# Inner values in a PSUM bank of their own, keys and y in one bank, and another order of accumulates, expert pieces and first tiles

## What is computed

```python
x = x + wkv(w, u, layernorm(x), ctx)     # a weighted running mean of ctx, weights exp(key)
h = layernorm(x)
shared = sigmoid(h @ sg.T) * ((silu(h @ Wg.T) * (h @ Wu.T)) @ Wd.T)     # inner width 1024
routed = sum over the 2 best of 8 experts of prob * expert(h)           # inner width 256 each
out = x + shared + routed
```

## Time and profile before

| | us |
|---|---|
| runs (3): median, lowest, highest | 590.62, 587.41, 590.75 |
| the profiled execution's own time | 590.7 |
| its span, first to last instruction | 588.8 |
| PE busy | 484.0 (82%) |
| DVE busy | 437.7 (74%) |
| POOL busy | 345.4 (59%) |
| ACT busy | 277.5 (47%) |
| mean granted TensorE clock | 0.96 of full speed |

### The profile page before, as it was taken

How to read it: one execution, slowest core, us unless ns; L and a number is a source line. 1 busy time by engine, 2 the same in 40 slices (tenths; PEclk the granted TensorE clock), 3 DMA queues, 4 the chain that set the end, 5 groups by cost and what they waited for, 6 DMA issues and landing times.

```text
span 588.8 us, 11209 instructions
## 1 busy us (share of the span) xinstructions
PE 484.0 (82%) x3293; PEld 319.8 (54%) x3293; DVE 437.7 (74%) x954; ACT 277.5 (47%) x534; POOL 345.4 (59%) x422
## 2 busy tenths in 40 slices
PE   0126828999899799899797998899999999999980
PEld 0025615766676677576575666555555555555530
DVE  5968787898989989989989677558665666666650
ACT  4687335357376375384573465543332323332320
POOL 5964346755857848848858264642455755565332
PEclk9999768999999999899899999999999999999995
DMA  7961111021322314213230501043547866766452
GB/s 284 409 255 37 40 32 36 20 90 38 127 91 73 131 50 159 76 56 127 72 125 7 162 20 48 2 127 73 103 85 140 146 113 114 128 119 111 89 72 36
DMA packets 25932, 59.21 MB, mean 101 GB/s; under 512 B 6314, under 2 KB 6314, under 8 KB 24338
## 3 DMA queue, kind: packets, MB, share of 16 engines
q0 software_dynamic: 9824, 20.90, 20.0%
q1 hardware_dynamic: 16050, 37.59, 17.9%
HBM read 37.83 MB, written 20.65 MB: 99 GB/s over the span
## 4 chain that ended last, share of the span: by engine, by line
PE 34%; DVE 24%; issue 12%; ACT 8%; DMA 6%; POOL 2%; SPq 1%; POOLq 0%; ACTq 0%; DVEq 0%
PE GU L956 13%; PE GU L995 6%; PE DN L971 6%; PE DN L1011 5%; DMA out<-wall,cb 5%; DVE hx L1313 3%; DVE wall L1192 3%; PE XT L902 3%; DVE st L1195 2%; DVE wall L1185 2%; ACT wall L736 2%; DVE th L1306 2%; DVE th L1308 1%; ACT wall L658 1%; PE YT L902 1%
## 5 line engine op out<-in xcount | busy, mean ns | idle before, releaser
L995 PE MATMUL GU<-xt,wall 128*128 128x256 f16 x1536 | 193.1, 279 | 4.8 <-DVE xt L1217 2.4
L995 PEld LDWEIGHTS GU<-xt,wall 128*128 128x128 f16 x1536 | 153.0, 101 | 40.3 <-issue 5.2
L1011 PE MATMUL DN<-wall,hx 128*128 128x512 f16 x384 | 100.0, 399 | 28.5 <-DVE xb L1320 16.1
L614 POOL DMA_INDIRECT out<-wall,cb x39 | 62.0, 1590 | 81.5 <-SPq L386 39.6
L683 ACT ACTIVATE th<-GU,scl 128x256 f32<-128x256 f32 x103 | 48.5, 471 | 107.3 <-PE GU L995 58.3
L1011 PEld LDWEIGHTS DN<-wall,hx 128*128 128x128 f16 x384 | 36.9, 101 | 69.5 <-issue 25.3
L1313 DVE TENSOR_TENSOR hx<-th,hx 128x256 f16<-128x256 f32 x64 | 47.6, 744 | 27.2 <-ACT hx L692 26.3
L1306 DVE SCALAR_TENSOR_TENSOR th<-th,GU 128x256 f32<-128x256 f32 x103 | 41.9, 407 | 31.4 <-ACT th L683 31.1
L956 PE MATMUL GU<-wall,kb 128*128 x240 | 61.4, 379 | 0.2 <-issue 0.2
L956 PE MATMUL GU<-wall,xnb 128*128 x228 | 58.5, 379 | 0.4 <-DVE xnb L1516 0.4
L971 PE MATMUL DN<-wall,hx 128*128 x234 | 56.9, 379 | 1.0 <-DVE hx L1313 1.0
(11 more groups left out here) (164 smaller groups left out, 809.1 us busy)
## 6 DMA issues: line engine op xcount, KB each, us to landing
wall<-wgu SPq DMA_DIRECT2D x12, 1024.0 KB, 7.7
wall<-wd SPq DMA_DIRECT2D x12, 512.0 KB, 8.5
out<-xb SPq DMA_DIRECT2D x20, 256.0 KB
xb<-x SPq DMA_DIRECT2D x16, 256.0 KB, 2.9
cb<-ctx_t SPq DMA_DIRECT2D x16, 256.0 KB
xn_rows<-xnb SPq DMA_DIRECT2D x16, 256.0 KB
xb<-xn_rows,cb POOLq DMA_INDIRECT x39
out<-wall,cb POOLq DMA_INDIRECT x39
```

Of the source, the lines that this page charges most:

```text
L614: pool.indirect_dma_start(out, bass.IndirectOffsetOnAxis(ap=idsa[:, j:j + 1], axis=0), ye[j % RESULTS], None, compute_op=ALU.add).then_inc ...
L995: ins = nc.tensor.matmul(GU[n % 2][:, g * 2 * P:(g + 1) * 2 * P], gate_up(sh_base(u // 2), wp, c)[:, f:f + P], xt_pair(n // PU * 2, xp, c) ...
L1011: ins = nc.tensor.matmul(DN[a][:], hx[n % 2][:, hp * IE + a * P:hp * IE + (a + 1) * P], down(sh_base(u // 2), wp, u % 2), start=u == 0 and ...
```

## The change

- A bank HS takes the inner values of the shared units: the second instruction of `hidden` writes HS instead of th, `unit_hi` and `hidden_lo` read HS. The slots' transposed inner values go to HS too. `unit_tanh` of a shared unit waits for `hidden` of unit n-2 instead of its `hidden_lo`.
- KT and YT are one bank. `keys_t` therefore waits for the residual of the tile before, `y_back` for the keys of the tile after. Tile 2's keys go to DN0.
- In the turns: `accumulate` stands right behind `residual_and_stats`; `keys_t` follows unit n+1 instead of unit n; `unit_hi(n+3)` stands behind the first expert piece of its own turn instead of at the head of the next turn. In turn 4 `y_back(3)` follows the first unit instead of standing inside it.
- The opening is in another order on all four engines.
- In the last shared groups some expert pieces and squares change places with `unit_hi`, and the low weights of expert 6 are made by DVE (two instructions) instead of POOL (three).

The diff, cut to its core (indentation shortened):

```diff
@@ -183,10 +183,14 @@
-KT, YT, XT, LG = bank("KT"), bank("YT"), bank("XT"), bank("LG")
+YT, XT, LG, HS = bank("YT"), bank("XT"), bank("LG"), bank("HS")
 GU = [bank("GU0"), bank("GU1")]
 DN = [bank("DN0"), bank("DN1")]
-HT = YT
+KT, HT = YT, HS
+
+def kt(t):
+    return DN[0] if t == 2 else KT
+
@@ -519,23 +523,20 @@
+    quotient(1)
...
-    quotient(1)
...
-    shared_d_lo(0)
...
+    shared_d_lo(0)
...
-    pool.wait_ge(nd, 4)
+    shared_d_lo(1)
...
-    shared_d_lo(1)
@@ -567,25 +568,23 @@
-    scatter(B - 4)
...
+    scatter(B - 4)
...
+    scales(E, E - 2)
+    scatter(B - 2)
...
-    scales(E, E - 2)
-    scatter(B - 2)
...
-    for k in range(3):
-        expert_lo(E - 2, k)
@@ -679,7 +678,7 @@
         act.wait_ge(gu, n + 1)
-        wait_from(act, h_lo, n - 1)
+        wait_from(act, h_rdy if n < N_EXP + 2 else h_lo, n - 1)
         nc.scalar.activation(th[par][:], GU[par][:, 0:IE], ACT.Tanh, scale=scale(row, TANH)).then_inc(tanh, 1)
@@ -689,7 +688,7 @@
         wait_from(act, dn, n - 1)
-        nc.scalar.activation(hx[par][:, 0:IE], th[par][:] if n < N_EXP else HT[:, 0:IE],
+        nc.scalar.activation(hx[par][:, 0:IE], HS[:, 0:IE] if n < N_EXP else HT[:, 0:IE],
                              ACT.Copy).then_inc(h_hi, 1)
...
@@ -750,45 +752,44 @@
-    first_norm(2)
...
+    first_norm(2)
+    expert_square(0, 0)
...
+    both_exps(2)
...
-    both_exps(2)
-    for k in range(3):
-        expert_square(0, k)
...
+    first_norm(3)
...
-    first_norm(3)
-    shared_d_split(0)
...
+    expert_square(0, 1)
...
-    shared_gu_hi(2)
+    shared_d_split(0)
...
+    shared_gu_hi(2)
+    unit_hi(1, 1)
+    shared_d_split(1)
...
+    unit_tanh(2, 0, SHARED)
...
-    shared_d_split(1)
-    unit_hi(1, 1)
...
-    unit_tanh(2, 0, SHARED)
...
-    both_exps(4)
-    first_norm(5)
...
+    both_exps(4)
+    first_norm(5)
+    unit_hi(3, 1)
+    expert_square(0, 2)
...
-        unit_hi(n - 1, 1)
@@ -815,10 +816,14 @@
-            for k in range(4):
+            expert_piece(hi_e, 0)
+        if ws_e is not None:
+            expert_piece(ws_e, 4)
+        unit_hi(n + 3, 1)
+        if hi_e is not None:
+            for k in range(1, 4):
...
-            expert_piece(ws_e, 4)
...
@@ -877,16 +880,18 @@
+    unit_hi(n + 2, 0)
...
-    unit_hi(n + 2, 0)
...
+    unit_hi(n + 3, 1)
...
-        unit_hi(N_EXP + j - 1, (N_EXP + 1 + r) % 2)
+        if j > 0:
+            unit_hi(N_EXP + j - 1, (N_EXP + 1 + r) % 2)
@@ -905,11 +910,14 @@
         wait_from(pe, kp1, t)
-        transposes(KT, kb, HC, k_t)
+        if t != 2:
+            wait_from(pe, x1_rdy, t - 1)
+        transposes(kt(t), kb, HC, k_t)
...
         wait_from(pe, x1_rdy, t)
+        pe.wait_ge(kp1, min(t + 2, B))
         transposes(YT, wkv(t, 3), HC, y_t)
@@ -1038,10 +1046,10 @@
+    sum_squares(1, 2 * SU + 1, 0)
...
-    sum_squares(1, 2 * SU + 1, 0)
+    y_back(1)
...
-    y_back(1)
@@ -1054,12 +1062,16 @@
     shared_units(0, beside={1: [first_turn_1], 2: [first_turn_2], 3: [lambda: xn_t_(2)]},
-                 beyond={0: [lambda: keys_t(3)]})
+                 between={0: [lambda: keys_t(3)]})
...
         def beside_0():
+            if i == LAG + 1:
+                y_back(i - 1)
             pe.wait_ge(listed, (i - 4) * LIST_STEPS + 2)
...
+
+        def beside_1():
             if i + 1 < B:
@@ -1069,7 +1081,7 @@
-        shared_units(j, between={0: [lambda: y_back(i - 1)]}, beside={0: [beside_0], 2: [beside_2]})
+        shared_units(j, between={0: [lambda: y_back(i - 1)]} if i > LAG + 1 else {}, beside={0: [beside_0], 1: [beside_1], 2: [beside_2]})
@@ -1132,7 +1144,7 @@
-            pe.wait_ge(last_lo, 1)
+            pe.wait_ge(last_lo, 2)
@@ -1167,7 +1180,7 @@
-        TT(wkv(t, 1), KT[:], growth[:], ALU.subtract).then_inc(kp1, 1)
+        TT(wkv(t, 1), kt(t)[:], growth[:], ALU.subtract).then_inc(kp1, 1)
@@ -1287,15 +1300,14 @@
-    def last_expert_lo(k):
...
-        e = E - 1
+    def last_expert_lo(e, k):
...
-            dve.wait_ge(w_hi, 3 * E)
+            dve.wait_ge(w_hi, 3 * e + 3)
...
-            dve.wait_ge(w_hi, 1 + 3 * E)
+            dve.wait_ge(w_hi, 3 * e + 4)
@@ -1305,12 +1317,12 @@
         dve.wait_ge(a1, n + 1)
-        STT(th[par][:], th[par][:], scale(row, KAPPA), GU[par][:, IE:2 * IE], ALU.mult,
+        STT(HS[:, 0:IE] if n < N_EXP else th[par][:], th[par][:], scale(row, KAPPA), GU[par][:, IE:2 * IE], ALU.mult,
             ALU.mult).then_inc(h_rdy, 1)
...
         dve.wait_ge(h_hi, n + 1)
-        TT(hx[par][:, IE:2 * IE], th[par][:] if n < N_EXP else HT[:, 0:IE], hx[par][:, 0:IE],
+        TT(hx[par][:, IE:2 * IE], HS[:, 0:IE] if n < N_EXP else HT[:, 0:IE], hx[par][:, 0:IE],
            ALU.subtract).then_inc(h_lo, 1)
@@ -1345,24 +1357,23 @@
+    first_stats(2)
...
-    first_stats(2)
...
-    reciprocals(1, 0, 2)
+    reciprocals(1, 0, HC)
...
-    reciprocals(1, 2, 2)
...
-    act_lo(0)
...
+    act_lo(0)
@@ -1370,31 +1381,28 @@
-    reciprocals(2, 0, 2)
+    reciprocals(2, 0, HC)
...
-    reciprocals(2, 2, 2)
+    hidden_lo(0, 0)
+    hidden(1, 1, SHARED)
...
-    hidden_lo(0, 0)
+    scan_e(3)
+    scan_ev(3)
+    hidden_lo(1, 1)
+    add_now(3)
+    residual_and_stats(2)
...
-    hidden(1, 1, SHARED)
...
-    scan_e(3)
-    scan_ev(3)
-    hidden_lo(1, 1)
-    add_now(3)
...
-    residual_and_stats(2)
...
+    first_stats(5)
...
-    first_stats(5)
@@ -1411,6 +1419,9 @@
         residual_and_stats(i - 1)
+        if j % 2 == 0:
+            accumulate(j - 2)
+            accumulate(j - 1)
         if i == LAG + 1:
@@ -1419,9 +1430,6 @@
         reciprocals(i, 0, 1)
-        if j % 2 == 0:
-            accumulate(j - 2)
-            accumulate(j - 1)
         hidden(n + 1, 1, SHARED)
@@ -1560,6 +1568,8 @@
     hidden_lo(n, 0)
+    last_expert_lo(E - 2, 0)
+    last_expert_lo(E - 2, 1)
     dve.wait_ge(ids_t, 1)
```

More of the change, by code:

```diff
@@ L863, in _ @@
             expert_piece(E - 2, 0)
+            unit_hi(n + 2, 0)
             expert_piece(E - 2, 1)
[L865 removed]
             unit_tanh(n + 3, 1, SHARED)
[L867 to L868 removed]
+            expert_piece(E - 2, 2)
+            unit_hi(n + 3, 1)
             n = N_EXP - SU
[L872 removed]
             unit_tanh(n, 0, SHARED)
```

25 lines of the change are left out of this document (12 added, 13 removed).

## The result

The changed kernel takes 557.8 us (median of 4 runs, 556.43 to 558.06) against 590.21 for the kernel before beside it (587.41 to 590.75). The ratio is 0.946, with an interval of 0.943 to 0.949. The forecast was 557.0. The profiled execution has a span of 555.6 us against 588.8.

The account below looks back on a forecast made before the run. TensorE and VectorE were taken as nearly full in the turns, with 5.4 us of TensorE stalls per pair. Opening -12, turns -19 and last shared stages -2.5 took 590.7 to 557 us; range 549 to 565, 8 in 10: 544 to 573.

Parts of the forecast that it names:

- Low halves from PSUM: Shared units: 64 low halves reading PSUM take 0.42 us beside GpSimd, so VectorE sheds 4.1 us per pair of turns.
- The write to PSUM costs nothing: Hidden steps of shared units: writing a VectorE result to PSUM was counted as free; upper bound 4.5 us of VectorE time.
- The rival that priced it at 0.7 us more each: Shared units' hidden steps: VectorE writes to PSUM are slow, 64 of them bring the kernel to 602 us; chance 0.03.
- Accumulates early: Turns: VectorE reaches accumulates earlier by 0.42 + about 1.8 us, covering TensorE's 2.72 us wait; new wait at most a few tenths.
- This only frees VectorE: Turns: high half of unit n+3 behind one expert piece, not four, removes VectorE's 1.26 us wait once a pair, nothing more.
- keys_t one unit later: Turns: in the bank shared with y, the later key transposes are covered; without that cover they cost 0.5 us a turn.
- The turns' sum: Turns 5 to 15: a pair goes from 40.4 to 36.8 us, eleven turns take 202.4, saving 19 us.
- Tanh(3), 7.7 us earlier: Opening: unit 3's tanh moved ahead of tile 4's exponentials and a norm, the largest term of the opening's sum.
- The rival saw the mechanism: Opening gives only its squares: tile 4's exponentials or expert weights hold y_back(3) where it was; 567 us, chance 0.12.
- No wait over 5 us: Opening, a sign of success: TensorE's third y_back waits at most 5 us and comes by about 78 us.
- The two waits named: Last shared stages: TensorE's 1.31 us wait at 337.07 and the 1.86 at 376.72 go; the stages give -2.5 us.
- the blocked reads move: Turns: GpSimd's reads block scans or adds instead, 1.3 us a turn, saving 4.7 instead of 19; 571 us, chance 0.15.

## Why the prediction came out, step by step

**Low halves from PSUM: right, and the central step.** The longest of 103 is 426 ns where "near 0.43" was asked for. In its size it depends on the accumulates' place: VectorE sheds 7.6 us in the turns with them early and 13.8 with them late, not the 4.1 a pair (22.6) that I summed. The kernel before has only four long low halves in its turns, not one in each pair, and ten short ones, 18.7 us in all. With the accumulates late the low halves give these 18.7, and 5.6 come back through the product of 128x16 elements (1.9 to 4.9 us) and L1260 (0.8 to 3.2).

**The write to PSUM costs nothing: right.** The hidden step takes 490 ns on average with HS as its result and 480 with th in the 39 slots: 64 x 10 ns = 0.6 us. The rival that priced it at 0.7 us more each is out. The Trainium skill, "VectorE: DVE Perf Modes", section "The TRN2 errata", has 62 more fixed cycles for a PSUM source; 103 low halves from PSUM at a median of 424 ns, against 64 from SBUF at 420 to 422, do not show it.

**Accumulates early: right only as a help against the blocks.** I counted it as a step of its own; with PSUM values it gives 0.4 us, less than can be told from nothing.

**"This only frees VectorE": wrong, the high half was undersized.** It is worth about 2.7 us in the turns and perhaps 3 after them. The step left out what TensorE waits for, the low half that follows the high half.

**keys_t one unit later: covered, as said.** The price without it was wrong fivefold: 0.5 a turn forecast, 27.4 / 11 = 2.5 measured. I had priced the late transposes alone, not the wait for y that sharing the bank turns into TensorE's.

**The turns' sum** was right within 2 us: 36.8 a pair forecast, 36.6 measured. The allowances lay differently: 0.1 us beyond the 17.5 in a turn without accumulates (0.5 allowed), 1.5 in one with them (1.3 allowed), part of it for the quotient, a wait not foreseen. Of the turns' 20.9 us, 14.0 are PSUM and accumulates together. Of the other 6.9, 5.8 lie in the turns without accumulates. The high half gives 2.7, but it was tested with the inner values in PSUM only, where nearly all of it lies in the turns with them. If the parts add, some 4 are not assigned.

**The opening: the sum right (-12.1 against -12) by luck, its terms wrong.** "Tanh(3), 7.7 us earlier" was the failed step: that move gives 0.7. What gave the time was the chain of tile 2 (3.5), the place of y_back(3) behind unit 4 (3.7, which I had not priced by itself), 2.25 from the first stages (2.5 forecast), and 2.9 behind y_back(3), with a higher granted clock, for which the sum had no term. The rival saw the mechanism: tile 4's exponentials do hold y_back(3), but at 79.68 and not at 85.52. "No wait over 5 us" and "by about 78" were missed by 0.3 and 1.7.

**Last shared stages (-2.1 against -2.5) and slots (+1.9 against 0).** The two waits named are gone as said. That the sum fits is partly luck: with the same code and full clock the stages take 51.4 to 51.7 us, so -3.7 to -4.0. Not foreseen were the wait of 3.04 behind the chain of small steps with the slow products after it, and the ScalarE order at the slots' start, which the diff shows; "nothing on the path is touched" was wrong by 1.4 us. The other 0.5 is within what the slots vary by.

**The rival "the blocked reads move"** happened in a small form: in eleven turns 4.9 us more on the product of 128x16 elements and 2.6 more on L1260, 0.7 a turn, not 1.3. The Trainium skill, "SBUF — State Buffer", section "Who interferes with whom", says that a VectorE instruction with two SBUF inputs contends with a GpSimd one that reads SBUF. This trace agrees even for a product of 16 columns: 1.30 us beside a GpSimd one of 1.27. No scan was held in the turns (1.22 us on average), but in the opening two were. The prediction had named held scans as a sign that it is wrong:

```profile
57.82 2.72 DVE L1188 TENSOR_TENSOR_SCAN wall<-by_time,wall 128x512 f32<-128x512 f32 x1
...
77.30 2.29 DVE L1188 TENSOR_TENSOR_SCAN wall<-by_time,wall 128x512 f32<-128x512 f32 x1
```

Together they cost VectorE 2.6 us that the opening's sum did not have. In the kernel before, the one at the second place takes 1.23 us.

## What to carry to other kernels

Where two engines are both nearly full, look first for single operations that take many times their usual time, and give them another source or target before moving work around them: moving the accumulates was worth 7 us with the blocks in place and nothing measurable once these were gone. When a buffer is shared between two users, the price is a new order between them; move the second user behind the first one's reader in the same edit, or it costs as much as all the rest gives (32.7 us of span here). And a term of a sum is not confirmed by the sum: the opening came out within 0.1 us with its largest term wrong by ten times.
